# A four-batch attention and expert kernel: head program, last pair and second-score masks rewritten

## What is computed

```python
x = x + ln(attn(ln(x)))          # ln: layer norm without weights
x = x + ln(ffn(ln(x)))

def attn(x):                     # 16 heads of 64, E = 128
    xn = layer_norm(x) * g + b
    q, k, v = heads(xn @ wq + bq), heads(xn @ wk + bk), heads(xn @ wv + bv)
    s = q @ k.T / 8
    s = where(key < query, -inf, s)      # a query sees its own and later keys
    return softmax(s) @ v @ w0 + b0 + x

def ffn(x):                      # 8 experts of rank 16, top 2 chosen by token 0
    gates = top2_softmax(x[:, 0] @ router.T)
    return x + (x @ down.T) * gates @ up
```

## Time and profile before

| | |
|---|---|
| median of 3 runs | 1035.44 us (1035.22 to 1038.36) |
| profiled execution, its own time | 1036.07 us |
| its span, first to last instruction | 1034.4 us |
| PE busy | 959.2 us (93%), 8533 matmuls |
| POOL busy | 703.5 us (68%) |
| DVE busy | 644.6 us (62%) |
| ACT busy | 537.7 us (52%) |
| mean granted clock of PE | 0.975 of full speed |

### The profile page before, as it was taken

One profiled execution on the slowest core, in us unless ns is written; L12 is line 12 of the kernel. 1 busy time (PEld: TensorE's weight loads), 2 busy tenths in 40 slices (PEclk: granted clock), 3 DMA queues, 4 the chain that ended last, 5 costly groups with the idle time before them and its releaser, 6 DMA issues.

```text
span 1034.4 us, 22143 instructions
## 1 busy us (share of the span) xinstructions
PE 959.2 (93%) x8533; PEld 623.6 (60%) x8533; DVE 644.6 (62%) x1924; ACT 537.7 (52%) x735; POOL 703.5 (68%) x505
## 2 busy tenths in 40 slices
PE   3699999999999999999999999999999999999972
PEld 1465665666666666666665666666666666666542
DVE  5656566565657667657657767656666665756354
ACT  4145654654444565665454564665455455564443
POOL 7057766686666767876567878776578676776752
PEclk9699999999999999999999999999999999999995
DMA  3000000101111101111100200110100200000101
GB/s 110 21 2 23 19 7 22 23 23 43 22 23 22 23 22 23 22 23 43 22 3 22 63 23 22 23 22 3 42 23 22 63 23 23 18 7 22 23 22 41
DMA packets 61816, 27.05 MB, mean 26 GB/s; under 512 B 39056, under 2 KB 53776, under 8 KB 61712
## 3 DMA queue, kind: packets, MB, share of 16 engines
q1 hardware_dynamic: 61712, 25.64, 10.6%
HBM read 22.76 MB, written 2.35 MB: 24 GB/s over the span
## 4 chain that ended last, share of the span: by engine, by line
PE 77%; DVE 10%; ACT 5%; POOL 3%; issue 3%; DMA 0%; POOLq 0%; ACTq 0%
PE po L634 21%; PE st L619 17%; PE sc L584 8%; PE st L673 5%; PE st L614 5%; PE st L551 4%; ACT ring L855 3%; DVE sc L1008 3%; PE sc L644 3%; PE st L608 3%; POOL total L420 3%; PE st L553 3%; PE st L552 3%; PE st L567 2%; PE st L568 1%
## 5 line engine op out<-in xcount | busy, mean ns | idle before, releaser
L420 POOL TENSOR_TENSOR total<-total,ring 128x1024 f32<-128x1024 f32 (+1 forms) x315 | 543.6, 1726 | 272.9 <-PE po L634 226.9
L1008 DVE CUSTOM_DVE_ANT_0 sc<-sc,key_mask 128x256 f32<-128x256 f32 (+3 forms) x512 | 237.8, 522 | 159.9 <-PE sc L584 156.3
L855 ACT ACTIVATE ring<-st 128x1024 f32<-128x1024 f32 (+1 forms) x256 | 228.8, 918 | 178.9 <-PE st L619 167.2
L1011 DVE TENSOR_REDUCE least<-sc 128x1 f32<-128x512 f32 x256 | 164.9, 686 | 77.1 <-PE sc L584 76.8
L634 PE MATMUL po<-ring,v_sb 128*64 128x512 f32 (+3 forms) x1280 | 210.6, 467 | 0.0
L619 PE MATMUL st<-q_high,k_low 64*128 64x512 f32 (+3 forms) x768 | 176.6, 447 | 0.0
L634 PEld LDWEIGHTS po<-ring,v_sb 128*64 128x64 f32 x1280 | 86.7, 137 | 128.5 <-issue 123.5
L584 PE MATMUL sc<-k_high,q_high 64*128 64x512 f32 (+3 forms) x768 | 136.1, 386 | 19.4 <-DVE least L1008 10.1
L619 PE MATMUL st<-q_low,k_high 64*128 64x512 f32 (+3 forms) x768 | 136.3, 342 | 0.0
L619 PE MATMUL st<-q_high,k_high 64*128 64x512 f32 (+3 forms) x768 | 136.2, 342 | 0.0
L584 PEld LDWEIGHTS sc<-k_high,q_high 64*128 64x128 f32 x768 | 69.3, 189 | 85.3 <-issue 63.9
(11 more groups left out here) (146 smaller groups left out, 1267.0 us busy)
## 6 DMA issues: line engine op xcount, KB each, us to landing
inv_row<-sums_dram SPq DMA_DIRECT2D x62, 256.0 KB, 4.0
x_a<-x SPq DMA_DIRECT2D x4, 512.0 KB, 5.2
sums<-sums_row SPq DMA_DIRECT2D x124, 2.0 KB, 2.1
x_b<-x SPq DMA_DIRECT2D x3, 512.0 KB, 5.7
out<-res_b SPq DMA_DIRECT2D x3, 512.0 KB, 4.6
ring<-w_pairs SPq DMA_DIRECT2D x1, 1152.0 KB, 6.6
shift_row<-shift_t SPq DMA_DIRECT2D x64, 4.0 KB
x_a<-x SPq DMA_DIRECT2D x2, 256.0 KB, 3.1
```

The lines of the kernel that those rows point to most:

```text
L420: nc.gpsimd.tensor_tensor(so_far, so_far, tile_of(n, s)[:, :, col:col + w], ALU.add).then_inc(s_add, 1)
L855: nc.scalar.activation(tile_of(n, s)[:, :, 0:w], st[s % 2][:, :, 0:w], ACT.Exp, scale=SCALE).then_inc(s_exp, 1)
L1008: last = nc.vector.tensor_tensor_reduce(bank[:, col:col + w], bank[:, col:col + w], key_mask[:, 0:w], -1.0, 3e38, ALU.add, ALU.min, least[ ...
L1011: last = nc.vector.tensor_reduce(least[:, h, a:a + 1], bank[:, col:col + w], AX.X, ALU.max, negate=True)
```

## The change

Four edits.

1. **Masks of the second scores.** Two products of depth 64 for each head and diagonal block (`mask_half[., a]` with `ident_half[., a]`, a = 0, 1) become one (`keys_before` with `which`). In pair 0 the same two tiles also mask the first scores by products, and DVE takes plain maxima there.
2. **Head.** Slots -2 and -1 are gone; an order of their own stands in their place, with the projection of pair 0 taken by halves, and the products of pair 1's projections put singly between first scores. Pair 0's `shifts` and `move_shift` stand ahead of the loops, and `turn_shift(0)` ahead of the first score of pair 1.
3. **First values.** Both parts of v of pair 0 move into stretch 0 of slot 0, behind its second scores, and so do first scores 1 and 2 of pair 1 (`FIRST_S_STEPS`, `FIRST_ORDER`).
4. **Tail.** The sums of the last pair come with tokens on partitions: DVE adds the exponentials up (`add_last`; POOL's adds of steps 4 and 5 of pair 31 go with it), PE makes them 16 columns of sums, DVE takes reciprocals of 8 values a partition. The two heads are projected apart and joined on DVE with the reciprocals as scalars (`take_out`). The two halves of the tokens go one ahead of the other, and DVE applies half of the tiles of a layer norm beside ACT (`apply_last`).

```diff
+            project(0, 0, range(0, 3)).then_inc(s_half, 1)
+            project(0, 0, range(3, 6)).then_inc(s_fill[1], 1)
+            project(1, 0, range(3, 6)).then_inc(s_half, 1)
+            project(1, 0, range(0, 3)).then_inc(s_fill[0], 1)
+            score(0, 0)
+            project(0, 1, range(0, 1))
+            score(0, 1)
+            project(0, 1, range(1, 2))
+            score(0, 2)
+            project(0, 1, range(2, 5))
+            score(0, 3)
+            project(0, 1, range(5, 6)).then_inc(s_fill[1], 1)
+            for s in range(4, 8):
+                score(0, s)
+                project(1, 1, range(s - 4, s - 3))
+            score(0, 8)
+            project(1, 1, range(4, 6)).then_inc(s_fill[0], 1)
+            fill(("m", 0, 0), "sc")
+            score(1, 0)
...
+    FIRST_S_STEPS = [(1, range(1, 5)), (1, range(5, 9)), (2, range(0, 3))]
+    FIRST_ORDER = ["TSTSTSS", "STSTTSTS", "STSTTS"]
...
             if t == 0:
-                found.insert(0, (("c0", 0, 0), "sc"))
+                found = [(("c0", 0, 0), "sc"), (("v", 0, 0), x), (("v", 0, 1), y)] + found
...
                 for i, (_, _, col, w, _) in enumerate(masked):
-                    for a in range(2):
-                        for h in range(2):
-                            nc.tensor.matmul(st[s % 2][:, h, col + w - P:col + w], mask_half[rows[h], a, :],
-                                             ident_half[rows[h], a, :], start=(i == 0 and a == 0), stop=False)
+                    for h in range(2):
+                        nc.tensor.matmul(st[s % 2][:, h, col + w - P:col + w], keys_before[rows[h], :], which[rows[h], :],
+                                         start=(i == 0), stop=False)
...
+            def last_half(a):
...
+                need(s_last_add, a + 1)
+                for j in range(4):
+                    for h in range(2):
+                        i = 8 * a + 2 * j + h
+                        last = nc.tensor.matmul(sc[:, 0, i:i + 1], added[a][:, h, j * P:(j + 1) * P], ones[:, 0:1],
+                                                start=True, stop=True)
+                last.then_inc(s_last_sum, 1)
...
+                        last = nc.tensor.matmul(by_head[a][h][:, j * P:(j + 1) * P], o_raw[(N - 1) % 2][rows, tokens],
+                                                w0_sb[rows, (N - 1) % PAIRS, :], start=True, stop=True)
+                last.then_inc(s_last_out, 1)
...
+            def out_before(a):
...
+                for t in range(4 * a, 4 * a + 4):
+                    last = nc.tensor.matmul(at_half(st[0], t), o_norm[:, t * P:(t + 1) * P], w0_sb[:, (N - 2) % PAIRS, :],
+                                            start=True, stop=True)
...
+                    if (t, g) == (N - 1, 2):
+                        last_half(0)
...
+            add_last(0)
+            add_last(1)
...
+            def take_out(a):
+                dve.wait_ge(s_last_sum, a + 1)
...
+                nc.vector.reciprocal(inverse[:, 8 * a:8 * a + 8], sc[:, 0, 8 * a:8 * a + 8]).then_inc(s_last_inv, 1)
...
+                for h in range(2):
+                    for j in range(4):
+                        i = 8 * a + 2 * j + h
+                        last = nc.vector.scalar_tensor_tensor(out=rows[:, j, :], in0=by_head[a][h][:, j * P:(j + 1) * P],
+                                                              scalar=inverse[:, i:i + 1], in1=rows[:, j, :], op0=ALU.mult,
+                                                              op1=ALU.add)
...
+                norm_stats(2, acc[b % 2], (low, high)[a]).then_inc(s_var, 1)
...
+            def apply_last(norm, a, src):
...
+                for t in range(4 * a + 2, 4 * a + 4):
+                    last = nc.vector.tensor_scalar(y_a[:, t, :], src[:, t, :], m[:, t, 2:3], m[:, t, 3:4], ALU.mult, ALU.add)
...
+            take_out(0)
+            residual(0)
+            take_out(1)
...
             take_logits(...); rank_logits(b); make_gate(b)
+            residual(1)
+            apply_last(3, 1, x_a).then_inc(s_last_u, 1)
```

More of the change, by code:

```diff
@@ L109, in sandwich_kernel, with place @@
     SPOT, BEFORE, holder = {}, {}, {}
-    for t in range(-2, N):
-        for g in range(3):
[L112 to L118, removed]
+    def place(user):
+        SPOT[user] = len(SPOT) % 3
+        BEFORE[user] = holder.get(SPOT[user])
+        holder[SPOT[user]] = user
+    for s in range(BLOCK_STEPS):
+        for h in range(2):
+            place(("S", 0, s, h))
+    place(("m", 0, 0))
+    for h in range(2):
+        place(("S", 1, 0, h))
+    for t in range(N):
+        for g in range(3):
+            ahead, blocks = firsts(t, g)
+            for s in blocks:
+                for h in range(2 * (t + ahead < N)):
+                    place(("S", t + ahead, s, h))
+            for use, bank in fills(t, g):
+                if bank == "sc":
+                    place(use)
     def halves(n, s, h):
@@ L538, in turn_four, with project @@
                 return last
-            def project(weight, n):
+            def project(weight, n, products=range(6)):
                 b, p = divmod(n, PAIRS)
@@ L584, in score @@
                         last = nc.tensor.matmul(banks[h][:, col:col + w], q_high[n % 3][rows[h], i * P:(i + 1) * P],
-                                                k_high[n % 3][rows[h], k0:k0 + w], start=True, stop=True)
+                                                k_high[n % 3][rows[h], k0:k0 + w], start=True,
+                                                stop=not (diagonal and by_products))
+                    for h in range(2 * (diagonal and by_products)):
+                        last = nc.tensor.matmul(banks[h][:, col:col + P], which[rows[h], :], keys_before[rows[h], :],
+                                                start=False, stop=True)
                 last.then_inc(s_score, 1)
@@ L920, in _, with take_half @@
             take_z(st[0][:, 1, :], slice(HALF, S))
+            def take_half(dst, weight, half):
+                tokens = slice(half * HALF, (half + 1) * HALF)
+                return nc.scalar.activation(dst[0][:, tokens], at("qk"[weight], 0, 0)[:, tokens], ACT.Identity,
+                                            bias=bias_col[:, 0, weight:weight + 1])
+            act.wait_ge(s_half, 1)
+            take_half(q_high, 0, 0)
+            wait_filled(act, "q", 0, 0)
+            take_half(q_high, 0, 1).then_inc(s_high, 1)
+            act.wait_ge(s_half, 2)
+            take_half(k_high, 1, 1).then_inc(s_later_keys, 1)
+            wait_filled(act, "k", 0, 0)
+            take_half(k_high, 1, 0).then_inc(s_high, 1)
+            for use in (("q", 1, 0), ("k", 1, 0), ("m", 0, 0)):
+                take(use, USE[use][0])
             for t in SLOTS:
-                c, i = divmod(t, PAIRS) if t >= 0 else (0, -1)
-                after = 1 <= c < B and t < N
+                c, i = divmod(t, PAIRS)
+                after = 1 <= c < B
                 for g in range(3):
@@ new lines, in apply_last, with residual @@
+            def apply_last(norm, a, src):
+                dve.wait_ge(s_root, last_root(norm, a))
+                m = moments[norm]
+                for t in range(4 * a + 2, 4 * a + 4):
+                    last = nc.vector.tensor_scalar(y_a[:, t, :], src[:, t, :], m[:, t, 2:3], m[:, t, 3:4], ALU.mult, ALU.add)
+                return last
+            def residual(a):
+                if a == 0:
+                    link(apply_last(2, a, acc[b % 2]))
+                dve.wait_ge(s_last_r, a + 1)
+                link(nc.vector.tensor_tensor(rows_of(x_a, a), rows_of(x_a, a), rows_of(y_a, a), ALU.add))
+                norm_stats(3, x_a, (low, high)[a]).then_inc(s_var, 1)
```

331 lines of the change are left out of this document (186 added, 145 removed).

## The result

The changed kernel took 1021.13 us (median of 4 runs, 1020.90 to 1022.29), the kernel before 1036.20 us (4 runs): a ratio of 0.985, 95% interval 0.984 to 0.986, so 15.1 us faster. 1012 was forecast, in a range of 1003 to 1021: the time lies at the very end of the range. The profiled execution of after has a span of 1020.6 us, 13.8 less than before; it was the longest of its four runs (1022.29 us, the others 1020.90 to 1021.31).

| stretch | before | after | gain | forecast |
|---|---|---|---|---|
| start to first values | 61.97 | 58.84 | 3.1 | 5.0 |
| first values to the end of T9 | 929.08 | 922.89 | 6.2 | 11.5 |
| T9's end to the end | 43.35 | 38.87 | 4.5 | 7.0 |

What follows compares the result with a forecast made beforehand. PE was taken to bound the 32 slots, latency the head and tail. Masks 11.5 + head 5.0 + tail 7.0 = 23.5 us off the median 1035.44 gave 1011.9, rounded to 1012; range 1003 to 1021 for 8 in 10.

Steps and rivals of the forecast that it cites:

- Masks: Second scores in the 32 slots: 1024 mask products become 512, 0.36 us a slot, 11.5 us; bounds 8 and 15.4.
- T3, T6, T7, T8 pay: Second scores: halved masks at these four places shorten the path by 0.06 + 0.12 + 0.06 + 0.12 = 0.36 us a slot.
- I take nothing off: 8 slots where T7 waits for DVE (7.9 us): no deduction, since that DVE work starts from a first score moved forward.
- The page's price: Slots: about 81 ns a matmul would give 0.97 us a slot, 31 us in all; 992 us had chance 0.02.
- Head: Start to first values: first T 12.3 us earlier, less 7.3 us in slot 0, gives 5.0 us; bounds 1.5 and 8.5.
- about 57: End of the head: first values of slot 0 start at about 57 us instead of 61.97.
- Tail: After T9 of the last slot: last add 7.6 us earlier, less 0.6 for POOL holding DVE, gives 7.0; bounds 3.5, 9.5.
- the DMA out is the same: End of the kernel: after the last add, at 1024.0 instead of 1031.63 us, the outgoing DMA takes as long as before.
- POOL held DVE: Rival, tail: joined adds and applications wait for POOL at two or three places, 2.2 us each; 1016 to 1019; chance 0.08.
- The masks paid: Judges the rival that masks don't pay, PE's shorter stretches ending in more waits for ACT; 1023.4 us; chance 0.08.
- The head gave 4.2 us: Judges the rival that the head gives nothing back, first scores waiting for DVE or shifts landing late; 1017; chance 0.06.
- DVE was not late in all slots: Judges the slower rival: k's low part late for T7 in all slots, 1.1 us in each other 24; chance 0.03.

Runs made afterwards that it cites:

- experiment 5: Changed kernel with batch 2's residual add moved behind the root of the first half's second norm: 1019.36 us; with v also in the head, 1017.02 us.

## Why the prediction was right in direction and 9 us too low

- **Masks, 11.5 us forecast, 7.4 alone in runs, 6.2 by the profile.** "T3, T6, T7, T8 pay" failed at T7. Doubling the masks of T5, T7 and T9 changed nothing, so all three are off the path; the first score behind T7 grows by what T7 loses. An ordinary slot lacks 0.08 us, 0.06 of it T7's. "I take nothing off" for the slots in which T7 waits for DVE failed too: slots 3, 9, 15, 17, 23 and 25 gain only 0.15 to 0.20 us, and 11, 19 and 24 nothing. In slot 11 DVE's L1085 is held to the end of a POOL add, `k_low` follows it, and POOL's adds stand as far behind the slot's start as before. There PE is not what sets the slot's length, and POOL was less free than I had read: 673 of 940 us is 72%, which leaves 28% and not "a third and more". Slot 16 gains nothing in the profile of after and 1.06 in that of the masks alone, which is the second hold of experiment 5; and slot 0 is 0.5 us longer, with edit 3's first scores in it, where the masks alone made it 0.3 shorter. These two, 1.9 us together, are why the slots gain 8.2 us in the profile of edit 1 alone and 6.2 in that of after.
- **The page's price.** The trace disagrees with the about 81 ns a matmul of the Trainium skill, TensorE: Matmul & The Clock Gate, section Back-to-back issue gap, after the change too: 512 instructions less gave 7.4 us, 14 ns each.
- **Head, 5.0 forecast, 3.1 by the profile, 4.2 in runs.** The first T came 1.8 us late (44.45, not 42.7): `least_of_two` ended at 40.4 instead of 38.2, and from there to the first T it took 4.1 us instead of 4.5. In eight other profiles with this head up to there it ended between 38.6 and 40.5, so part of this is the spread told of below. From the first T to the first values it took 7.4 us more than before. The forecast had 7.3, but 0.6 of that (a first score and a stall in stretch 1) lies behind the first values, so its "about 57" did not follow from its own terms; 56.4 did. Half speed cost 2.8 us (T0 to T2 with 1.28, 1.28 and 1.11 us for 0.70, and the same for what lies between), not 1.7: this term was sized too small. PE's waits for DVE in stretch 0 came to 1.2 us, where 1.3 was forecast, and the fills of v to 2.9, where 3.2 was.
- **Tail, 7.0 forecast, 4.5 by the profile, 4.4 in runs.** Statistics behind T9: 6.1 us instead of 5.5, for the most part since a joining instruction took 0.286 us (2.29 for 8), not 0.22; the sixteen one-column products took 1.9 us, not 1.3, which cost 0.1. The hold of L1085 cost 1.0 us, for which 0.6 stood in the sum; it was at one place, and moving POOL's add took it away. The other 1.5 us are 0.7 in many small steps up to the last add, and 0.8 from the last add to the end, 3.55 us in this profile and 2.73 before. The last DMA took 3.1 us from issue to landing there, and 2.3 before. In the other profiles with this tail the stretch is 3.2 to 3.5 us in seven and 2.7 in three, so "the DMA out is the same" does not hold for most; the cause stays open.
- **Rivals.** POOL held DVE once in the tail, for 1.0 us, not two or three times. The masks paid, for 7.4 us. The head gave 4.2 us by the medians. DVE was not late in all slots.
- **The size.** All three terms came out below the forecast and none above, and the range just reaches the result. The path was right for T3, T6, T8, the new head and the new tail; what failed is T7, the slots that other engines set, and the sizes of the slow clock, of the joining instructions and of the end.
- **Contention.** The rule of the Trainium skill, GPSIMD Engine Reference, section 1. Specifications, that instructions with two SBUF inputs contend, had no row before. Now it has, and the trace agrees: the first add of `add_last(0)`, 1.01 us of it beside a POOL add, took 2.10 us, and the last, of the same size and with none beside it, 1.23:

```profile
975.06 1.28 POOL L455 TENSOR_TENSOR total<-total,ring 128x512 f32<-128x512 f32 x1 [0.17 <-POOL total L455]
975.33 2.10 DVE L1249 TENSOR_TENSOR total<-ring 128x1024 f32<-128x1024 f32 x1 [0.34 <-ACT ring L928]
...
978.91 1.23 DVE L1249 TENSOR_TENSOR total<-total 128x1024 f32<-128x1024 f32 x1
```

## What to carry to other kernels

Of instructions taken from the bound engine count only those behind which that engine meets no wait; doubling them one group at a time shows it cheaply. A shorter period does not help a slot whose length is set by a chain on other engines. Before a few us between two kernels are called the work of an edit, cut both spans into the same stretches: here 2.1 of 3.2 us lay where nothing had been changed.

## What was not expected of the hardware

- A DVE instruction on 128x4 values that starts beside a POOL add ends with it (0.17 us becomes up to 2.38 in after); so it was in 17 of 40 places before and in 18 after. Whether a second one slips in between two POOL adds made 1.1 us of slot 16. It went both ways with its recorded start within 0.03 us of the add's.
- The head is not the same from execution to execution. With a head that no edit touched, the first values stood at 57.38 to 58.84 us in six profiles. The kernel with the masks alone has the head of before and stood at 65.68 instead of 61.97 in its profile: 1.2 us of that are there at the first maximum (25.63 for 24.39), 1.9 by the first T (56.86 for 55.00), and the rest comes behind it, where six products of T0 and of T1 took 1.28 us each instead of 0.70. The granted clock was lower, as the windows show (before, then masks alone). So 3.1 us for the head by two profiles is worth less than the 4.2 by medians.

```profile
50.00:60.00 10.00, 9.37 (x60) 0.76 0.15 44
```
```profile
50.00:60.00 10.00, 8.02 (x36) 0.55 0.19 55
```

- Sixteen one-column products of 128x128 weights (L705) took 1.95 us from the first start to the last end, one every 0.112 us, as much as with 128 columns (0.111 in L673 of before).
